# Cross-attention of a decoder layer: the row maxima turned by transposes in place of products with the identity

## The reference

```
q = (x @ w_q).reshape(b, n, 16, 64)
k, v = halves of (context @ w_kv), reshaped alike
attn = softmax(einsum('bnhd,bmhd->bhnm', q, k) * 64 ** -0.5)
out  = einsum('bhnm,bmhd->bnhd', attn, v).reshape(b, n, 1024) @ w_out + b_out
x = layernorm(x + out)
```

## Time and profile before

| | |
|---|---|
| median of 3 runs | 1907.34 us (1907.2 to 1907.8) |
| the profiled execution | 1908.62 us |
| its span, first to last instruction | 1906.9 us |
| PE, PEld busy | 1720.8 us, 1201.1 us |
| DVE, ACT, POOL busy | 1148.3 us, 841.2 us, 1241.7 us |
| mean granted TensorE clock | 0.940 of full |

### The profile page before, as it was taken

One profiled execution on the slowest core, in us unless ns is written; L12 is line 12 of the kernel. 1 busy time (PEld: TensorE's weight loads), 2 busy tenths in 40 slices (PEclk: granted clock), 3 DMA queues, 4 the chain that ended last, 5 costly groups with the idle time before them and its releaser, 6 DMA issues. The chain is left out here.

```text
span 1906.9 us, 31047 instructions
## 1 busy us (share of the span) xinstructions
PE 1720.8 (90%) x10604; PEld 1201.1 (63%) x10604; DVE 1148.3 (60%) x2045; ACT 841.2 (44%) x1208; POOL 1241.7 (65%) x703
## 2 busy tenths in 40 slices
PE   6654699999999999999999999999999999747992
PEld 4543566666667666666666666766666665436991
DVE  4776455656565656666565656565666656466664
ACT  3223234444464444445444445464444445432223
POOL 3867238686676766766768677686676676325554
PEclk8776789999999999999999999999999999868996
DMA  6001300000120000012000000120000001132224
GB/s 199 1 23 30 125 1 23 1 24 0 57 58 23 1 23 1 23 53 60 23 1 23 1 23 0 69 45 23 1 23 23 0 16 38 62 122 75 76 78 144
DMA packets 39987, 75.96 MB, mean 40 GB/s; under 512 B 4728, under 2 KB 28664, under 8 KB 38592
## 3 DMA queue, kind: packets, MB, share of 16 engines
q1 hardware_dynamic: 35264, 59.27, 9.2%
q0 software_dynamic: 4608, 15.15, 3.1%
HBM read 55.97 MB, written 13.52 MB: 36 GB/s over the span
## 5 line engine op out<-in xcount | busy, mean ns | idle before, releaser
L1186 POOL TENSOR_TENSOR xa_total<-xa_total,xa_pexp 128x1024 f32<-128x1024 f32 (+1 forms) x337 | 818.2, 2428 | 63.8 <-ACT xa_pexp L1098 33.6
L1275 DVE TENSOR_REDUCE xa_parts<-ps_ring 128x1 f32<-128x402 f32 x1024 | 530.6, 565 | 260.8 <-PE ps_ring L1018 253.8
L1098 ACT ACTIVATE xa_pexp<-ps_s 128x1024 f32<-128x1024 f32 (+1 forms) x416 | 426.5, 1026 | 348.1 <-PE ps_s L972 312.4
L986 PE MATMUL ps_pv<-xa_pexp,xa_v 128*64 128x512 f32 (+1 forms) x1664 | 399.8, 604 | 0.0
L986 PEld LDWEIGHTS ps_pv<-xa_pexp,xa_v 128*64 128x64 f32 (+1 forms) x1664 | 105.9, 137 | 182.4 <-issue 147.2
L972 PE MATMUL ps_s<-xa_q_neg,xa_row_one 64*128 64x512 f32 (+1 forms) x832 | 183.4, 392 | 0.0
L1186 POOL TENSOR_TENSOR xa_total<-xa_pexp 128x1024 f32<-128x1024 f32 x31 | 74.1, 2389 | 151.3 <-ACT xa_pexp L1098 149.7
L1158 ACT COPY xa_v<-ps_ring 128x256 f32<-128x256 f32 (+1 forms) x208 | 77.5, 373 | 206.3 <-PE ps_ring L957 204.4
L1018 PE MATMUL ps_ring<-xa_k_hi,xa_q_hi 64*128 64x402 f32 x512 | 127.4, 377 | 14.0 <-DVE xa_parts L1275 13.4
L1018 PE MATMUL ps_ring<-first_k_hi,xa_q_hi 64*128 64x402 f32 x512 | 122.5, 388 | 3.3 <-DVE xa_q_lo L1269 1.5
L1330 DVE RECIPROCAL xa_inv<-xa_sums 128x128 f32<-128x128 f32 x124 | 116.9, 943 | 0.0
(11 more groups left out here) (302 smaller groups left out, 3350.3 us busy)
## 6 DMA issues: line engine op xcount, KB each, us to landing
wa_raw<-in_pack_a SPq DMA_DIRECT2D x17, 768.0 KB, 4.3
ex_raw<-in_pack_e SPq DMA_DIRECT2D x8, 1024.0 KB, 6.6
ctx_raw<-in_ctxT SPq DMA_DIRECT2D x4, 1601.0 KB, 7.8
first_ctx_lo<-ctx_raw POOLq DMA_DIRECT2D x6, 800.5 KB, 6.0
wb_raw<-in_pack_b SPq DMA_DIRECT2D x16, 256.0 KB, 2.6
ex_w<-ybuf SPq DMA_DIRECT2D x8, 512.0 KB, 7.4
sa_xT<-in_xT SPq DMA_DIRECT2D x8, 256.0 KB, 6.1
X<-in_x SPq DMA_DIRECT2D x1, 2048.0 KB, 11.2
```

What stands on the lines that cost most here:

```text
L986: ins = nc.tensor.matmul(ps_pv[half(h), :], v[0:m, t, at:at + XD], pexp[0:m, buf, h, :], start=t == 0, stop=t == MT - 1)
L1098: nc.scalar.activation(pexp[0:m, buf], ps_s[0:m, (p * MT + t) % 2], ACT.Exp, scale=XD ** -0.5)\
L1186: engine.tensor_tensor(total[p][0:m], first, pexp[0:m, buf], ALU.add).then_inc(s["add_done"], 1)
L1275: nc.vector.tensor_reduce(parts[:, h, q, c:c + 1], ps_ring[:, r, 0:CW], AX.X, ALU.max)\
```

## The change

In step SH the four products of a square of `negmax` with the identity are replaced by four transposes of the same squares into the same places. Waits, semaphores, the bank, and everything before and behind are the same.

```
                     pe.wait_ge(s["maxima_in"], 2 * (n.of("SH") + 1))
                     for q in range(NC):
 
-                        ins = nc.tensor.matmul(ps_ring[:, r, q * P:(q + 1) * P], negmax[:, q, :], ident[:],
-                                               start=True, stop=True)
+                        ins = nc.tensor.transpose(ps_ring[:, r, q * P:(q + 1) * P], negmax[:, q, :], ident[:])
                     ins.then_inc(filled[r], 1)
```

## The result

| | before | after |
|---|---|---|
| median, same chip | 1907.57 us (4 runs) | **1894.06 us** (1893.28 to 1896.82, 4 runs) |
| ratio, 95% interval | | 0.993 (0.9917 to 0.9942) |
| profiled execution, span | 1908.62 us, 1906.9 us | 1896.82 us, 1895.1 us |
| mean granted TensorE clock | 0.940 | 0.937 |

The kernel became 13.5 us faster, with 16.3 us forecast and a range of 1889.2 to 1894.8 us. The profiled execution is the slowest of its four: its own gain is 11.8 us.

A forecast was written before the change was run, and what follows sets the result against it. PE was taken to bound the kernel; 15.0 us from 30 inner SH steps, 0.80 from the first and 0.47 from the last make 16.3 us, so 1907.34 becomes 1891.0 us, with a range of 1889.2 to 1894.8 us.

The forecast's parts named there:

- What bounds the kernel: Between 256 and 1594 us PE sets the pace, covered for 1334.82 of 1338 us; time it saves comes off the end.
- The inner steps: 30 SH steps between 256 and 1594 us at full clock, 0.50 us won in each, 15.0 us together.
- The two bounds: Gain of an inner SH step: 0.33 us by the self-attention's transposes (TX), 0.56 us by the experts' transposes.
- the experts' row: Among the experts a 128-row product begins 0.36 us after the first of four transposes; corrected to 0.42 us for SH.
- The first step: First SH, in the opening at half clock: 1.91 us of products become 1.11 us of transposes, 0.80 us won.
- The last step: Last SH, alone on the path in the last round: its group shrinks from 1.13 to 0.66 us, 0.47 us won.
- A quarter of the price: Rival at every SH: a transpose takes a quarter of its product's time, 22.8 us won, 1884.5 us; chance 2%.
- A later rise in the opening: Rival: transposes in the first SH delay the clock's rise by 3.4 us, 1.7 us lost, 1892.7 us; chance 6%.
- The clock falling at each SH: Rival: each SH costs 3.4 us at half clock, 1.7 us lost each; with all 31, 1943.7 us; chance 3%.
- Given back in the last round: Rival: POOL's chain begins at a fixed time, so PE's 12.51 us wait swallows earlier gains; 1906.9 us; chance 3%.

The follow-up runs named there:

- experiments 5 and 4: Kernel before with the last SH alone by transposes: 1910.29 us (1.000); changed kernel with four SH steps turned twice: 1894.67 us (0.9926 against before).
- experiment 3: Changed kernel with each square turned twice, so eight transposes for each SH: 1912.72 us (1.0004 against the kernel before).
- experiment 6: 84 idle products put into PE's long wait of the last round, in both kernels: before 1914.24 us (1.0027), changed 1897.94 us (0.994).

## Why the prediction was right, and where it was off

- **What bounds the kernel: right.** All of the 30 inner gains reached the end of the long wait (14.70 + 0.50 us). The stretch after, all engines, for the earlier trace rows:

```profile
257.30:1579.00 1321.70, 1318.42 (x8358) 879.06 (x8358) 807.62 (x1422) 659.78 (x903) 949.47 (x397) 1.00 0.07 22
```

- **The inner steps: right.** 0.50 us forecast, 0.507 measured. The two bounds were 0.33 and 0.56, and the choice of the experts' row, corrected for the first weight load, gave 0.42 us for four transposes where 0.41 to 0.42 were measured.
- **The first step: mis-sized,** 0.48 us measured for the 0.80 of the sum. SH was cut from 1.91 us to 1.06, and the distance to its successor from 1.57 to 0.71:

```profile
254.88 1.06 PE L1026 MATMUL ps_ring<-ident,xa_negmax 128*128 128x128 f32 x4
255.59 1.02 PE L957 MATMUL ps_ring<-first_ctx_hi,first_wb_hi 128*128 128x402 f32 x2
```

But the clock's rise comes 2.0 us behind the start of SH in both, at 256.01 and 256.91 us. So the products behind SH began earlier but ran longer at half clock, and the time won there counts half.
- **The last step: mis-sized.** SH itself gives 0.49 to 0.51 us (experiments 5 and 4), as forecast. But the sum took the clock in the last round as given. The 15.7 us won before moved the end of PE's wait to an unfavourable place, and the late rise cost 3.4 us. Without it the sum is 0.48 + 15.20 + 0.51 = 16.2 us, for the 16.3 forecast; with it 12.8 us, which is what the two profiles show from the first SH to RS (1425.93 against 1413.14). The medians have 13.5 and 13.75. Where the other 0.7 to 1.0 us lie is not shown: the two profiles of before themselves differ by 1.6 us up to the first SH and by 3.2 us behind RS.
- **The rivals.** A quarter of the price: refuted by experiment 3. A later rise in the opening: it did not come, with transposes in half of the 2 us before it. The clock falling at each SH: it stood at 1.00 throughout the long stretch, in which 30 groups of transposes lie. Both of these rivals reckon with 3.4 us, for which they show no row; experiment 6 has two stretches at half clock of that length, and in the last round a rise came 9 us later. Given back in the last round: the mechanism named there (POOL's chain at a fixed time) was wrong, as the wait kept its 12.5 us and moved with PE. But the place was the right one: a fifth of the gain was given back there, by the clock.
- **The range held in part by luck,** near its high end, because the late rise in the opening (1.7 us) had been put into it for the clock. The case that came was twice as dear and elsewhere, and the forecast itself, 1891.0 us, was 3.1 us too low. A chance for it could have been had from the trace of before: behind PE's wait of 12.51 us the clock was at half there already, until 1638.41 us, and nothing said that it would come back as early when the wait ended at another time.

## What to carry to other kernels

A product of an f32 square with the identity cost 0.22 us here and its transpose 0.11 us, and on an engine that is covered all the time half a microsecond in 32 places arrived almost whole. Price such a change by the distance to the successor, not by the records' durations. And before counting on the sum, look for stretches at half clock between the change and the end: time won ahead of them moves the work against the clock's changes, and can win or lose some us (here 3.4) that belong to no instruction. A variant with a little more work, ahead of such a stretch and profiled, is then the test that tells it from the change itself.

## What the runs showed of the hardware that I had not expected

- Less work, later end: the changed kernel takes 1411.29 us from the first SH to RS with 1.75 us of added transposes, 1413.14 and 1412.86 without, and the late rise, which costs 3.4 us, is the reason.
- A DVE addition of 128x1024 f32 took 4.35 us beside a POOL subtraction of 3.42 us, and 1.22 us at the median on a quiet POOL. The two spans overlap from 1610.78 to 1614.05 us, and 1614.05 + 1.22 = 1615.27 is where the addition ended (1615.13), as if it had only begun then. The kernel before has such a case in its last block: beside a POOL subtraction that ended at 1652.51 us an addition of DVE took 3.23 us, and it ended at 1653.60. The Trainium skill (SBUF — State Buffer, section Terms, "shared port pair") says that DVE and GpSimd share one pair of read and write ports to SBUF, which an instruction holds for its whole time while the other engine waits; both rows agree.
- Eight transposes follow each other as evenly as four, 0.11 us each, and the rise of the clock came 4.5 us behind the wait with transposes in the last SH where it came 4.3 and 4.4 us behind it with products.
